# Self attention with two-bank maximum slots, single-bank exponentials, and the weighing of values between the second and the third score matmul

## The reference, cut to what matters

```python
q = (src @ q_w).reshape(b, s, h, hd).transpose(0, 2, 1, 3)
k = (src @ k_w).reshape(b, s, h, hd).transpose(0, 2, 1, 3)
v = (src @ v_w).reshape(b, s, h, hd).transpose(0, 2, 1, 3)
scores = jnp.einsum('bhqd,bhkd->bhqk', q, k) / np.float32(np.sqrt(hd))
scale = jax.nn.sigmoid(jnp.einsum('bhsd,hd->bhs', q, scale_w)) * 2.0
scores = scores * scale[..., None]
aw = jax.nn.softmax(scores, axis=-1)
out = jnp.einsum('bhqk,bhkd->bhqd', aw, v).transpose(0, 2, 1, 3).reshape(b, s, d)
```

## Time and profile before

| | |
|---|---|
| median of 3 runs | 2311.32 us |
| the profiled execution | 2307.65 us |
| its span | 2306.0 us |
| first A matmul of the self attention | 392.97 us from the span's start |
| first B matmul | 438.33 us |
| last transpose of a sum (the end of the self attention on PE) | 1258.29 us |
| busy over the whole span | PE 1817.1, DVE 1374.1, ACT 915.9, POOL 490.2 us |

### The profile page before, as it was taken

The page is one execution under the profiler, slowest core; times in us unless marked ns, Lnnn a source line. Parts: engine busy times, 40 slices in busy tenths (PEclk is TensorE's granted clock), DMA queues, the critical chain, the costliest instruction groups (busy, mean ns, idle before and its releaser), DMA issues. The chain is left out here.

```text
span 2306.0 us, 32650 instructions
## 1 busy us (share of the span) xinstructions
PE 1817.1 (79%) x10156; PEld 858.1 (37%) x10157; DVE 1374.1 (60%) x2819; ACT 915.9 (40%) x1188; POOL 490.2 (21%) x518
## 2 busy tenths in 40 slices
PE   5899795899999999999997782599337996114997
PEld 3466462222222222222221561377224663002564
DVE  5344353888788787888882353376585545584221
ACT  3323263266566565666666330244224332001110
POOL 4200153300000000000000343433563001037343
PEclk8999897699999999999999885799769998656998
DMA  4000188111111112111100305322210004201352
GB/s 123 1 2 1 56 292 247 33 34 34 35 34 34 35 46 55 34 34 34 34 1 27 133 0 170 111 65 63 66 30 1 2 2 138 91 0 37 92 127 29
DMA packets 111993, 137.16 MB, mean 59 GB/s; under 512 B 14176, under 2 KB 88032, under 8 KB 111584
## 3 DMA queue, kind: packets, MB, share of 16 engines
q1 hardware_dynamic: 97008, 113.33, 16.7%
q0 software_dynamic: 9216, 16.79, 3.2%
q10 hardware_dynamic: 5616, 5.11, 0.7%
HBM read 78.31 MB, written 56.89 MB: 59 GB/s over the span
## 5 line engine op out<-in xcount | busy, mean ns | idle before, releaser
L948 DVE TENSOR_REDUCE sa_mpart<-sa_a 128x1 f32<-128x512 f32 x1024 | 653.6, 685 | 142.3 <-PE sa_a L1034 134.6
L1016 ACT ACTIVATE sa_e<-sa_b 128x1024 f32<-128x1024 f32 x512 | 499.2, 1022 | 313.1 <-PE sa_b L1061 313.0
L1034 PE MATMUL sa_a<-sa_k,sa_q 96*128 96x512 bf16 x1024 | 386.8, 404 | 59.8 <-DMA sa_k<-k_parts 26.7
L1061 PE MATMUL sa_b<-sa_q,sa_k 98*128 98x512 bf16 x1024 | 310.6, 386 | 9.3 <-issue 6.8
L1071 PE MATMUL sa_ops<-sa_e,sa_v 128*17 128x512 f32 x2048 | 273.3, 604 | 0.0
L1034 PEld LDWEIGHTS sa_a<-sa_k,sa_q 96*128 96x128 bf16 x1024 | 87.6, 97 | 451.8 <-DVE sa_mpart L948 406.1
L1173 POOL TENSOR_TENSOR ao_var<-ao_mv,x_eps_pow 128x4 f32<-128x4 f32 x8 | 1.6, 203 | 905.2 <-DVE ao_mv L1272 905.2
L1061 PEld LDWEIGHTS sa_b<-sa_q,sa_k 98*128 98x128 bf16 x1024 | 97.0, 99 | 107.0 <-issue 39.0
L213 DVE TENSOR_REDUCE xa_mx<-xa_rows 128x16 f32<-128x1024 f32 x64 | 78.3, 1223 | 97.9 <-PE xa_rows L445 97.9
L360 ACT ACTIVATE xa_pT<-xa_cols 128x1024 f32<-128x1024 f32 x64 | 62.1, 1022 | 84.9 <-PE xa_cols L477 84.9
L2454 DVE TENSOR_TENSOR sw_hT<-sw_p,sw_act 128x512 f32<-128x512 f32 x32 | 22.1, 691 | 107.8 <-PE sw_p L2399 92.8
(11 more groups left out here) (325 smaller groups left out, 2773.8 us busy)
## 6 DMA issues: line engine op xcount, KB each, us to landing
sa_q<-q_parts SPq DMA_DIRECT2D x16, 768.0 KB, 6.0
sa_k<-k_parts SPq DMA_DIRECT2D x16, 768.0 KB, 8.9
tc_w<-in_L_ffn_W SPq DMA_DIRECT2D x24, 512.0 KB
k_parts<-sp_kpart SPq DMA_DIRECT2D x16, 384.0 KB, 2.9
q_parts<-sp_qpart SPq DMA_DIRECT2D x16, 384.0 KB, 2.9
expert_in<-ao_zero SPq DMA_DIRECT2D x1, 4992.0 KB, 22.6
expert_out<-ex_xb ACTq DMA_DIRECT2D x39, 128.0 KB, 1.7
v_groups<-sp_vt SPq DMA_DIRECT2D x8, 544.0 KB, 3.6
```

The costliest lines, as they stand in the source:

```text
L948: nc.vector.tensor_reduce(mpart[par][:, head, rest // 2, rest % 2:rest % 2 + 1], aps[k % 2][:], axis=X, op=ALU.max).then_inc(max_done, 1)
L1016: nc.scalar.activation(ex[kt % 2][p][:], bps[p][:], ACT.Exp, scale=SCALE).then_inc(exp_done, 1)
L1034: nc.tensor.matmul(aps[k % 2][:], qs[s][0:KROWS, head, q0:q0 + P], ks[s][0:KROWS, head, (rest % 2) * CW:(rest % 2 + 1) * CW], start=True, ...
L1061: last = nc.tensor.matmul(bps[p][:, head % 2], ks[s][:, head, kt * P:(kt + 1) * P], qs[s][:, head, qc * CW:(qc + 1) * CW], start=True, sto ...
```

## The change

PSUM is divided anew: four banks for first scores (two slots `aps` of two banks), three single banks `bps` for second scores, one for `ops`, and none for `misc`.

- A slot of first scores now has both halves of the keys of one head and query tile: two matmuls, and one maximum over 1024 columns (`maximum`). `combine` and its tile `mpart` are gone.
- The two transposes take turns with the first scores in the same two slots. Every filling of a slot is numbered (a use); a use waits until DVE is done with the use two before it (`fill`, semaphore `a_used`). A unit has 18 uses: 16 maxima, one transpose of maxima, one of the sum.
- A second-score matmul writes one bank and is released by itself, and ACT takes exponentials of 512 columns, 32 of them a unit where there were 16 of 1024. The three banks rotate, so a B matmul waits for the exponential three before it.
- On PE a key tile is: B, a slot (two A), B, the V of the key tile before, B, a slot (two A), B. V waits for all four exponentials of its key tile. The V of a unit's last key tile stands in the first key tile of the next unit, and ACT's copy of the sum after the third exponential of the next unit (`keep_out`).
- First scores run less far ahead: in key tiles 0 and 1 the last four slots of unit n+1, in the other six the first twelve of unit n+2 (`ahead`). Before the first unit there are 28 slots where there were 32 pairs. The transpose of maxima stands after key tile 2.
- Group 0 is written out ahead of the loop, then the loop over three groups passes four times, then three groups are written out. The waits that were satisfied in advance by memsets are left out for the first unit.

The diff, cut to its core:

```diff
     SETS = 3
+    TILE_MAXIMA = GH * CT
+    EARLY = TILE_MAXIMA - 4
+    FIRST = TILE_MAXIMA + 1 + EARLY
+    USES = TILE_MAXIMA + 2
...
-        ex = [[sb(f"e{i}{p}", [P, 2, CW]) for p in range(2)] for i in range(2)]
-        mpart = [sb(f"mpart{i}", [P, GH, CT, 2]) for i in range(2)]
-        mfull = sb("mfull", [P, GH, CT])
+        ex = [sb(f"e{i}", [P, GH, CW]) for i in range(2)]
+        mfull = [sb(f"mfull{i}", [P, GH, CT]) for i in range(2)]
...
-        bps = [ps(f"b{p}", [P, 2, CW]) for p in range(2)]
-        aps = [ps(f"a{i}", [P, CW]) for i in range(2)]
+        bps = [ps(f"b{i}", [P, CW]) for i in range(3)]
+        aps = [ps(f"a{i}", [P, 2, CW]) for i in range(2)]
         ops = ps("ops", [P, CW])
-        misc = ps("misc", [P, CT, P])
...
+        def ahead(n, kt, which):
+            a, k = (n + 1, EARLY + 2 * kt + which) if kt < 2 else (n + 2, 2 * (kt - 2) + which)
+            return None if isinstance(a, int) and a >= UNITS else (a, k)
...
+                def maximum(par, k, use, at):
+
+                    dve.wait_ge(a_filled, use + 1)
+                    nc.vector.tensor_reduce(mfull[par][:, k // CT, k % CT:k % CT + 1], aps[at][:].rearrange("p a b -> p (a b)"),
+                                            axis=X, op=ALU.max).then_inc(a_used, 1)
...
+                for k in range(TILE_MAXIMA):
+                    maximum(0, k, k, k % 2)
+                split_max(0, TILE_MAXIMA, 0)
+                for k in range(EARLY):
+                    maximum(1, k, TILE_MAXIMA + 1 + k, (TILE_MAXIMA + 1 + k) % 2)
...
+                def keep_out(n):
+
+                    act.wait_ge(pv_done, KT * n)
+                    act.wait_ge(a_filled, out_use(n - 1) + 1)
+                    nc.scalar.activation(o_sb[:], ops[:], ACT.Copy).then_inc(o_evacuated, 1)
+
+                def body(g, turn, s, turn1, s1):
                     for qc in range(2):
                         n = 2 * g + qc
-                        for kt in range(KT):
-                            for p in range(2):
-                                act.wait_ge(b_scores, 16 * n + 2 * kt + p + 1)
-                                act.wait_ge(pv_done, 16 * n + 2 * kt + p + 1)
-                                nc.scalar.activation(ex[kt % 2][p][:], bps[p][:], ACT.Exp, scale=SCALE).then_inc(exp_done, 1)
-                        act.wait_ge(pv_done, 16 * (n + 1) + 4)
-                        act.wait_ge(o_psum, n + 1)
-                        nc.scalar.activation(o_sb[:], ops[:], ACT.Copy).then_inc(o_evacuated, 1)
+                        for i in range(GH * KT):
+                            kt, head = i // GH, i % GH
+                            if head == 0 and later(n, 1) or kt >= 2 and head == 0:
+                                act.wait_ge(pv_done, KT * n + kt - 1)
+                            act.wait_ge(b_scores, GH * KT * n + i + 1)
+                            nc.scalar.activation(ex[kt % 2][:, head], bps[(2 * (2 * s + qc) + i) % 3][:], ACT.Exp,
+                                                 scale=SCALE).then_inc(exp_done, 1)
+                            if i == 2 and later(n, 1):
+                                keep_out(n)
...
+                def fill(use):
+                    if later(use, 2):
+                        pe.wait_ge(a_used, use - 1)
...
+                    q0 = (qc * CT + t) * P
+                    for half in range(2):
+                        last = nc.tensor.matmul(aps[at][:, half], qs[s][0:KROWS, head, q0:q0 + P],
+                                                ks[s][0:KROWS, head, half * CW:(half + 1) * CW], start=True, stop=True)
+                    last.then_inc(a_filled, 1)
+
+                def transpose_max(par, use, at, maxima):
+                    pe.wait_ge(a_used, maxima)
+                    nc.tensor.transpose(aps[at][0:GH * CT, 0, 0:P], mfull[par][:].rearrange("p h t -> p (h t)"),
+                                        ident[:]).then_inc(a_filled, 1)
...
+                def transpose_out(n, use, at):
+
+                    if later(n, 1):
+                        pe.wait_ge(o_evacuated, n)
+                    fill(use)
...
+                    if later(n, 1) or i >= 3:
+                        pe.wait_ge(exp_done, GH * KT * n + i - 2)
+                    nc.tensor.matmul(bps[(2 * (2 * s + qc) + i) % 3][:], ks[s][:, head, kt * P:(kt + 1) * P],
+                                     qs[s][:, head, qc * CW:(qc + 1) * CW], start=True, stop=True).then_inc(b_scores, 1)
+
+                def weigh_values(n, kt, s, turn):
+                    if kt == 0:
+                        if later(n, 1):
...
+                    pe.wait_ge(exp_done, GH * (KT * n + kt + 1))
+                    for head in range(GH):
+                        last = nc.tensor.matmul(ops[32 * head:32 * head + VW], vs[s][:, kt, head], ex[kt % 2][:, head],
                                                 start=(kt == 0), stop=(kt == KT - 1))
                     last.then_inc(pv_done, 1)
...
                         for kt in range(KT):
-                            scores(n, kt, 0, j, qc)
-                            ahead(4 * kt)
-                            scores(n, kt, 1, j, qc)
-                            ahead(4 * kt + 1)
-                            if kt:
-                                for p in range(2):
-                                    weigh_values(n, kt - 1, p, j, turn)
-                            ahead(4 * kt + 2)
-                            ahead(4 * kt + 3)
-                            if kt == 1 and not (known and n + 1 >= UNITS):
-                                transpose_max(n + 1)
+                            for head in range(GH):
+                                scores(n, GH * kt + head, s, qc)
+                                if head == 1:
+                                    if kt:
+                                        weigh_values(n, kt - 1, s, turn)
+                                    elif qc:
+                                        weigh_values(n - 1, KT - 1, s, turn)
+                                    elif later(g, 1):
+                                        weigh_values(n - 1, KT - 1, (s - 1) % SETS, turn)
+                                if head in (0, 2) and ahead(n, kt, head // 2):
+                                    a, k = ahead(n, kt, head // 2)
+                                    if kt < 2 and qc == 0:
+                                        first_scores(k, base + offset, at(offset), s, turn, 1)
+                                    else:
+                                        first_scores(k, base + offset, at(offset), s1, turn1, 0 if kt < 2 else qc)
+                                    offset += 1
+                            if kt == 2 and not (isinstance(n, int) and n + 1 >= UNITS):
+                                transpose_max((qc + 1) % 2, base + offset, at(offset), max(base + 4, base + offset - 1) if isinstance(n, int) else base + 5)
+                                offset += 1
                             if kt == 3:
-                                transpose_out(n)
-                        for p in range(2):
-                            weigh_values(n, KT - 1, p, j, turn)
-
-                for a in range(2):
-                    for k in range(AM):
-                        first_scores(a, k, 0, 0, a)
-                    if a == 0:
-                        transpose_max(0)
+                                transpose_out(n, base + offset, at(offset))
+                                offset += 1
+
+                for k in range(TILE_MAXIMA):
+                    first_scores(k, k, k % 2, 0, 0, 0)
+                transpose_max(0, TILE_MAXIMA, 0, TILE_MAXIMA)
+                for k in range(EARLY):
+                    use = TILE_MAXIMA + 1 + k
+                    first_scores(k, use, use % 2, 0, 0, 1)
                 pe.wait_ge(ones_made, SETS + 2)
                 groups(pe, body)
-                transpose_out(UNITS)
+                weigh_values(UNITS - 1, KT - 1, (GROUPS - 1) % SETS, (GROUPS - 1) // SETS)
+                transpose_out(UNITS, out_use(UNITS), out_use(UNITS) % 2)
```

More of the change, by code:

```diff
@@ L909, in pass_max @@
                                  m_dram[ds(a, 1)].rearrange("a r (h t) q -> r (a h) (t q)", h=GH)).then_inc(m_loaded, 16)
-                def body(g, turn, j):
-                    for qc in range(2):
-                        n = 2 * g + qc
-                        if qc == 0 and not (isinstance(g, int) and g + 2 >= GROUPS):
-                            sp.wait_ge(pv_done, 16 * n + 4)
-                            load(g + 2, turn, (j + 2) % SETS)
-                        a = n + 1
-                        if not (isinstance(a, int) and a >= UNITS):
-                            pass_max(a, (j + (a_is_next(qc))) % SETS, (qc + 1) % 2)
-                def a_is_next(qc):
-                    return 1 if qc == 1 else 0
-                load(0, 0, 0)
-                load(1, 0, 1)
+                def body(g, turn, s, turn1, s1):
```

(48 more changed lines are left out.)

126 lines of the change are left out of this document (59 added, 67 removed).

## The result

The changed kernel takes 2292.22 us, the median of 4 runs (2291.63 to 2294.94), against 2311.05 before (4 runs, 2309.53 to 2311.67): a ratio of 0.9922, 95% interval 0.9905 to 0.9939. It is 18.8 us faster; the forecast was 2293. The sum was right, but not all of its terms. In the two profiles the self attention takes 25.7 us less instead of 18.5 and ends 27.3 us earlier, and the rest of the program, which is the same code, takes 12 us more.

The account below looks back on a forecast made before the run. PE was taken as nearest to the bound, with waits on top of its work. Terms of -11 (thirty units), -10.5 (start) and +3 (last units and end) made -18.5 us, from 2311.3 to 2293 us; 8-in-10 range 2277 to 2308.

Parts of the forecast that it names:

- What bounds: Self attention: PE is nearest to the bound, 23.15 us of work in a 25.36 us unit, the rest waits.
- the three new waits: PE in a unit: 0.94 us after the transpose of maxima, 0.61 after the sum's, 0.29 at V in the second key tile.
- The unit: Self attention unit with first scores beside it: 24.99 us against 25.36, so -11 us over thirty units.
- The check on the order before: The same walk through PE's order in the kernel before gives 25.35 us a unit, against the measured 25.36.
- The last two units: Units without first scores: V waits for the last exponential, 2.59 us a key tile; +2.7 for the last, +0.8 for the other.
- The very end: End of the self attention, counted with the units lacking first scores: -0.3 us.
- The jumps: Three jumps back of the loop: DVE starts the body as late as before; 0, within 2 us either way each.
- The stretch before the first unit: First scores before the first unit, at 1.2 GHz and bound by the slots: -10.5 us, first B near 428.
- Rival 1: Slots after the transposes: no waits, a unit takes 23.4 us, the total 2245 us; chance 0.09.
- Rival 2: V in every key tile waits for the exponential; 25.8 us a unit, the total 2321 us; chance 0.10.
- Rival 3: DVE's two-bank maximum is no cheaper than two, 1.37 us; 25.45 us a unit, total unchanged at 2311; chance 0.09.
- Rival 4: PE's clock falls to 1.2 GHz in the units, adding 84 us over thirty, total 2377 us; chance 0.03.

## Why the prediction was right

**What bounds.** PE's work of 23.15 us a unit and what it waits for, not DVE's throughput: shown by the run with the moved transposes, which does the same DVE work and is 1.2 us a unit shorter, and by the two maxima in a slot, which add some 0.15 us of DVE work to each of 16 slots and cost 0.13 a unit. (The terms of that sum, as the prediction gives them, make 23.13.) Where the plain key tile lost its wait for DVE, 3.13 us became 2.82; the three new waits take back most of that.

**The unit.** 24.99 forecast, 24.92 measured. All three waits are at their places and close to their sizes: 0.93, 0.60 and 0.22 for 0.94, 0.61 and 0.29. The small rest is ACT: a 512-column exponential follows the one before at 0.49 us (three in 1.58 by the timeline), not 0.535. The prediction had the overlap of two exponentials from a pair of 1024 columns in 1.98 us. Four in a row in the same kernel took 3.77, which is one every 0.92, and the same overlap on 597 ns would have given 0.49. The check on the order before, 25.35 against the measured 25.36, is given without its working.

```profile
980.98 1.58 ACT L1035 ACTIVATE sa_e<-sa_b 128x512 f32<-128x512 f32 x3
```

and in the kernel before:

```profile
1221.04 3.77 ACT L1016 ACTIVATE sa_e<-sa_b 128x1024 f32<-128x1024 f32 x4
```

**The last two units.** V to V 2.55 us (1216.46 to 1219.01) against 2.59, and it is the chain of two exponentials that sets it. With the copy of the sum the last unit takes 20.98, for 21.25 forecast:

```profile
1216.46 1.05 PE L1092 MATMUL sa_ops<-sa_e,sa_v 128*17 128x512 f32 x8
...
1217.89 0.60 PE L1073 MATMUL sa_a<-x_ident,sa_o 128*128 128x128 f32 x4
...
1219.01 1.05 PE L1092 MATMUL sa_ops<-sa_e,sa_v 128*17 128x512 f32 x8
...
1230.98 0.66 PE L1073 MATMUL sa_a<-x_ident,sa_o 128*128 128x128 f32 x4 [0.72 <-ACT sa_o L1025]
```

**The very end** was mis-sized: -0.3 forecast, +2.1 measured. The V at 1219.01 is the first behind the last unit's transposes of a sum, and the last V, at 1229.21, is four steps of 2.55 behind it. Before, the first three steps took 6.36 and the last V followed the one before it at once:

```profile
1248.78 1.05 PE L1071 MATMUL sa_ops<-sa_e,sa_v 128*17 128x512 f32 x8
...
1255.14 2.45 PE L1071 MATMUL sa_ops<-sa_e,sa_v 128*17 128x512 f32 x16
```

The prediction priced a key tile of the last unit at 2.59 but didn't carry that price on to the key tiles behind the last transposes, where the same chain of exponentials holds. It shows no working for the -0.3.

**The jumps** were mis-sized: 0 forecast, -5.6 measured, 1.9 each and so just inside the 2 us either way that was allowed. The step said that DVE starts the body as late as before. DVE idles 2.0 to 3.0 us at the six jumps of the changed kernel's two profiles, and mostly for PE; before it was 2.9 to 4.6 at six. PE's second wait, 1.49 us in the earlier trace rows, is gone, and the clock is at 1.2 GHz for 10.2 us over the three jumps instead of 23.8, which by the prices above accounts for the difference. That the missing wait is what kept the clock up is likely and not shown. Why DVE was later before is not shown either; its loop body had twice as many maxima.

**The stretch before the first unit** gained 11.5, not 10.5. The prediction's own terms there (394.1 + 32.9 + 1.4) put the first B at 428.4, which is 9.9 and not 10.5, so it was off by 1.6. The first unit gained 1.9 more: PE was at 1.2 GHz for 4.5 us between the first B and the first transposes of a sum, where before it was 9.3.

**The rest of the program** was taken as unchanged. It is, but for the clock: 12 us more in the profile compared, and 27.3 became 15.3 in the span. That the total came out within 1 us of the forecast is luck to that extent: the gain of the self attention was reckoned 7 us too small, and by the medians the stages around it, which are the same code, took about as much more.

**The rivals.** Rival 1, no waits at the slots, falls, since the waits are there. Rival 2, V waiting in every key tile, does not happen at 0.49 an exponential; the run with V behind the first score matmul shows how near it is. Rival 3, a maximum of 1.37 us, falls with 1221 ns. Rival 4, the clock, falls too: the granted clock is 1.00 in the units, before and after. The rule of the Trainium skill (TensorE: Matmul & The Clock Gate, "A second HAM failure mode: psum-queue depth-cycling"), a clock that swings with short waits between bank-cycled matmuls, is not borne out by this trace, with 1.75 us of such waits in a unit at a clock of 1.00.

## What to carry to other kernels

When two kinds of result take turns in the same pair of buffers, look at what stands just ahead of the odd one: moving a small transpose from behind a freshly filled slot to behind a long piece of work was worth more than the change itself (36 us of the self attention against 26). A walk through one period of the order, with start intervals from the trace, gave each wait to 0.1 us; check it first on the kernel before. And compare stages, not totals, where the clock of later, unchanged stages moves the total by more than the effect.

## What was not expected of the hardware

- The program behind the self attention varied by 14 us over twelve profiles, and with it PE's time at 1.2 GHz (387 to 414 us).
- A jump back of the loop left PE idle for 2.2 to 2.6 us in the kernel before and the changed one, even where nothing was awaited. Written out, the changed kernel's units cost 0.09 us more each and no jump.
- A jump cost 2.2 to 2.5 us where the clock stayed up, 5.2 to 5.9 where it was at 1.2 GHz for 6.8 us behind the jump, and up to 6.7 where that lasted 10.2 us.
- 512-column exponentials of 600 ns each followed one another at 0.49 us, 1024-column ones of 1022 ns at 0.92 to 0.96.
